# Plain attention with a second, transposed score product in place of transposes of P, and batches pipelined

## The reference

```python
h = _layernorm(x, ln1_g, ln1_b)
q = (h @ Wq).reshape(Bb, Ss, H, Dh)      # k and v alike
scores = jnp.einsum('bqhd,bkhd->bhqk', q, k) / jnp.sqrt(jnp.float32(Dh))
attn = jax.nn.softmax(scores, axis=-1)
ctx = jnp.einsum('bhqk,bkhd->bqhd', attn, v).reshape(Bb, Ss, Dd)
x = x + ctx @ Wo
m = _layernorm(x, ln2_g, ln2_b)
...
probs = jax.nn.softmax(xt @ Wg, axis=-1)          # 8 experts, the best 2 of them
h1 = jax.nn.gelu(jnp.einsum('td,edf->etf', xt, W1) + b1[:, None, :])
ye = jnp.einsum('etf,efd->etd', h1, W2) + b2[:, None, :]
...
return x + moe_out                                 # then a last layer norm
```

## Time and profile before

| | us |
|---|---|
| median of 3 runs | 3999.53 (3998.75 to 3999.96) |
| span of the profiled execution, the one time given of it | 4001.5 |
| PE busy | 2997.8 (75%) |
| PE weight loads | 1922.9 (48%) |
| DVE busy | 2299.1 (57%) |
| ACT busy | 1970.1 (49%) |
| POOL busy | 912.2 (23%) |

### The profile page before, as it was taken

One profiled execution on the slowest core, in us unless ns is written; L12 is line 12 of the kernel. 1 busy time (PEld: TensorE's weight loads), 2 busy tenths in 40 slices (PEclk: granted clock), 3 DMA queues, 4 the chain that ended last, 5 costly groups with the idle time before them and its releaser, 6 DMA issues. The chain is left out here.

```text
span 4001.5 us, 63435 instructions
## 1 busy us (share of the span) xinstructions
PE 2997.8 (75%) x19516; PEld 1922.9 (48%) x19517; DVE 2299.1 (57%) x5064; ACT 1970.1 (49%) x3070; POOL 912.2 (23%) x614
## 2 busy tenths in 40 slices
PE   4757676676757575859779797887979079999990
PEld 2434334343434353437556575655757045556560
DVE  5868586868676777746566565665656211111116
ACT  3838484857566575725446464554645022222220
POOL 3525252625343534400000000000000410000006
PEclk7565656555655555555555656556565589999995
DMA  1010010101010101050000000000000410000005
GB/s 43 11 21 18 14 25 8 31 7 33 7 32 7 32 2 38 1 204 8 19 10 17 12 11 18 11 17 8 15 16 8 149 45 29 29 27 28 29 26 169
DMA packets 124051, 123.84 MB, mean 31 GB/s; under 512 B 28737, under 2 KB 116434, under 8 KB 123730
## 3 DMA queue, kind: packets, MB, share of 16 engines
q1 hardware_dynamic: 116578, 102.46, 9.5%
q0 software_dynamic: 6144, 16.79, 1.3%
q10 hardware_dynamic: 1008, 0.54, 0.0%
HBM read 46.22 MB, written 35.65 MB: 20 GB/s over the span
## 5 line engine op out<-in xcount | busy, mean ns | idle before, releaser
L369 POOL TENSOR_TENSOR TT<-MC,TT 128x1280 f32<-128x1280 f32 x112 | 341.2, 3082 | 269.6 <-ACT TT L404 269.6
L1034 PE MATMUL PTPb<-ident,PR 128*128 128x128 f32 x1376 | 381.1, 431 | 3.1 <-ACT PR L962 3.1
L962 ACT ACTIVATE PR<-sP,nm 128x512 f32<-128x512 f32 x512 | 348.3, 683 | 36.5 <-DVE nm L1136 34.3
L1136 DVE TENSOR_REDUCE nm<-sP 128x1 f32<-128x512 f32 x512 | 346.3, 680 | 32.6 <-PE sP L1026 32.6
L1141 DVE TENSOR_TENSOR PLb<-PTPb,PHb 128x512 f16<-128x512 f32 x344 | 237.9, 691 | 200.3 <-ACT PHb L968 200.0
L521 PE MATMUL SeP<-STG 48*128 48x128 f16 (+3 forms) x512 | 227.0, 443 | 144.7 <-DVE mn L705 141.1
L1026 PE MATMUL sP<-STGb 48*128 48x512 f16 x512 | 302.8, 600 | 40.5 <-DMA STGb<-HIb 40.4
L511 PE MATMUL mP<-STG 48*128 48x512 f16 (+3 forms) x512 | 179.4, 452 | 193.8 <-DVE MC L694 105.1
L968 ACT ACTIVATE PHb<-PTPb 128x512 f16<-128x512 f32 x344 | 205.5, 597 | 233.4 <-PE PTPb L1034 232.7
L705 DVE CUSTOM_DVE_ANT_0 TT<-SeP,TT 128x128 f32<-128x128 f32 (+3 forms) x512 | 248.2, 491 | 125.6 <-PE SeP L523 110.5
L1034 PEld LDWEIGHTS PTPb<-ident,PR 128*128 128x128 f32 x1376 | 244.4, 215 | 149.2 <-issue 137.6
(11 more groups left out here) (270 smaller groups left out, 7016.0 us busy)
## 6 DMA issues: line engine op xcount, KB each, us to landing
rows_scratch<-PR SPq DMA_DIRECT2D x1, 9216.0 KB, 28.6
X<-rows_scratch SPq DMA_DIRECT2D x72, 128.0 KB, 2.0
results_scratch<-X SPq DMA_DIRECT2D x72, 128.0 KB, 1.7
STG<-HI SPq DMA_DIRECT2D x128, 64.0 KB, 2.3
STG<-HI SPq DMA_DIRECT2D x256, 32.0 KB, 2.0
STG<-LO SPq DMA_DIRECT2D x256, 32.0 KB, 2.0
W1S<-in_L_ffn_W SPq DMA_DIRECT2D x8, 1024.0 KB, 16.7
W2S<-in_L_ffn_W SPq DMA_DIRECT2D x8, 1024.0 KB, 11.9
```

The lines of the kernel that those rows point to most:

```text
L369: pool.tensor_tensor(TT[:, g % 2, j, :], MC[:, g % 2, j, :], TT[:, g % 2, j, :], ALU.add).then_inc(sum_ready, 1)
L962: act.activation(PR[:, tc % RING, :], sP[tc % 4][:, :], ACT.Exp, bias=nm[:, tc % RING:tc % RING + 1]).then_inc(bp_ready, 1)
L1034: mm = pe.transpose(PTP[tc % 3][:, k * P:(k + 1) * P], PR[:, tc % RING, k * P:(k + 1) * P], ident[:, :])
L1136: dve.tensor_reduce(nm[:, tc % RING:tc % RING + 1], sP[tc % 4][:, :], AX.X, ALU.max, negate=True).then_inc(nm_ready, 1)
```

## The change

All of the second stage is written anew, and a few lines of the third.

- Row tiles are counted through all batches. One written-out loop over slots (n) on every engine takes the place of the loops over batches. A step is TP = 8 slots and belongs to two heads, one in each half of the partitions; 64 steps are 512 tiles. Every slot has one score product for the maxima and, LAG = 40 slots later, one transposed score product. The other work of a batch stands at fixed steps and slots before or after its tiles (`USES`, `at_batch`): norm 1 at step -13 to -11, q and k at -8 and -7, staging at -6 to -4, v at -2, the output product at 18 to 20, norm 2 at 22, the router at 24. A batch's steps are eight, so these fall among the tiles of other batches.
- The score product (48 rows) only serves the row maximum (DVE). Per group of four heads (16 slots), PE transposes the 16 columns of maxima, DVE divides them by 256 and splits them into two float16 rows, and SP writes them to DRAM and from there as two more rows below q in STG, opposite rows of 256 below k. The transposed product then has AUG = 50 rows, k as stationary and q moving, and gives scores less the maximum with the keys in the partitions. ACT's exponential of it writes PT, the transposed P, as float32. There is no transpose of P and no splitting into float16 parts.
- The product with v has blocks of PT (128x128 float32) as stationary operand and v (float32, 17 columns) moving, one logical product a block, in four bursts of 16 products a group, at slots 0, 2, 4 and 6 of every second step.
- All of SP's staging is twelve DMAs a batch by way of a copy of the parts in DRAM. The high and low parts of q and k are made on POOL out of a float32 copy by ACT. Norm 1's and norm 2's gain and bias are applied by ACT on the transposed rows (per partition), in the third stage too, where the copy of the transposed rows becomes two instructions.
- SP issues the 9 MB of zeros behind the staging of batch 0. W1's load moves from the second stage's start to the third's, ahead of W2's.

The diff, cut to its core (most removed lines are in the listing above):

```diff
--- before.py
+++ after.py
@@ -779,90 +779,111 @@
 
 
 
-        W1S = sb(top, "W1S", [P, E, CH, F])
         LG = sb(top, "LG", [P, N, E])
-        w1_loaded = sem("w1_loaded")
+        gcol = sb(top, "gcol", [P, 4, CH])
         with ExitStack() as ctx:
+            NP = H // 2
+            TP = 2 * NT
+            PAIRS = B * NP
+            GROUPS = B * NG
+            TILES = PAIRS * TP
+            LAG = 5 * TP
+            AUG = R3 + 2
+            SHIFT = 256.0
+            RT = NT // 2
+
...
+            VS = sb(ctx, "VS", [P, 2, NT, H, 32])
+            PT = sb(ctx, "PT", [P, 4, 2, NT, T])
...
+            shift_d = nc.dram_tensor("shift_scratch", [2, 2, 2 * TP, P], F16, kind="Internal").ap()
+            planes_d = nc.dram_tensor("planes_scratch", [2, 2, 2 * CH, P, T], F16, kind="Internal").ap()
...
+            BEGIN = slot(-15, 0)
+            END = slot(NP * (B - 1) + 26, 0)
+
...
+            USES = [("h", 0, -11, 0), ("h", 1, -11, 4), ("q", 0, -8, 1), ("q", 1, -8, 5), ("q", 2, -7, 1), ("q", 3, -7, 5),
+                    ("v", 0, -2, 0), ("v", 1, -2, 4), ("y", 0, 18, 2), ("y", 1, 18, 6), ("w", 0, 19, 4), ("w", 1, 20, 0),
+                    ("m", 0, 23, 0), ("m", 1, 23, 4), ("l", 0, 24, 7)]
...
+                    for n in range(BEGIN, END):
+                        g = at_group(n, 2, 7)
+                        if g is not None:
+                            sp.wait_ge(nmr_done, g + 1)
+                            b, p0 = g // NG, 2 * (g % NG)
+                            if g >= 2:
+                                sp.wait_ge(shifted[g % 2], 32 * (g // 2))
+                            sp.dma_start(shift_d[g % 2].rearrange("r c t -> c r t"), NMR[:, g % 2, :, :]).then_inc(nm_stored, 16)
+                            sp.wait_ge(nm_stored, 16 * (g + 1))
+                            for par in range(2):
+                                row = 64 * par + R3
+                                sp.dma_start(STG[row:row + 2, b % 2, 0, p0:p0 + 2, :],
+                                             shift_d[g % 2, :, TP * par:TP * par + TP, :].rearrange("r (q i) t -> r q (i t)", q=2)).then_inc(shifted[g % 2], 16)
+                        b = at_batch(n, -6, 0)
+                        if b is not None:
+                            if b >= 2:
+                                sp.wait_ge(staged[b % 2], 192 * (b // 2))
+                            sp.wait_ge(blo, 4 * b + 4)
+                            sp.dma_start(planes_d[b % 2, 0].rearrange("u p t -> p u t"), HI[:, :, :]).then_inc(pl_stored, 16)
+                            sp.dma_start(planes_d[b % 2, 1].rearrange("u p t -> p u t"), LO[:, :, :]).then_inc(pl_stored, 16)
+                        for half in range(2):
...
+                                par = half
+                                for jj, planes in [(0, (0, 0)), (1, (0, 1)), (2, (1, 0))]:
+                                    for qk in range(2):
+                                        src = planes_d[b % 2, planes[qk], 2 * qk:2 * qk + 2].rearrange("c (hh r d) t -> r d (c hh) t", r=2, d=D)
+                                        dst = 64 * par + D * jj
+                                        sp.dma_start(STG[dst:dst + D, b % 2, qk, :, :], src[par]).then_inc(staged[b % 2], 16)
+                                if b == 0 and half == 1:
+                                    sp.dma_start(xs_d.rearrange("s p c -> p s c"), Z[:, :].unsqueeze(1).broadcast_to([P, SLOTS, C])).then_inc(zeroed, 16)
...
+                    pool.memset(VS[:, :, :, :, :].rearrange("p s i h d -> p (s i h) d")[:, :, D:32], 0.0).then_inc(b_set, 1)
+                    pool.memset(Z[:, :], 0.0).then_inc(b_set, 1)
+                    for par in range(2):
+                        pool.wait_ge(b_set, 2 + par)
+                        pool.memset(STG[64 * par + 32:64 * par + 64, :, 1, :, :], SHIFT).then_inc(b_set, 1)
+                    pool.wait_ge(b_set, 4)
+                    pool.memset(VS[:, :, :, :, :].rearrange("p s i h d -> p (s i h) d")[:, :, D:D + 1], 1.0).then_inc(b_set, 1)
...
+                                    pool.wait_ge(pl_stored, 32 * b)
+                                pool.wait_ge(bank_out, nth["q", u, b] + 1)
+                                pool.tensor_copy(HI[:, u, :], QF[:, u, :]).then_inc(bhi, 1)
+                                pool.wait_ge(bhi, 4 * b + u + 1)
+                                pool.tensor_tensor(LO[:, u, :], QF[:, u, :], HI[:, u, :], ALU.subtract).then_inc(blo, 1)
...
+                        if 0 <= x < TILES:
+                            p, kt, par = x // TP, x % TP // 2, x % 2
+                            if x % TP == 0 and p >= 4:
+                                act.wait_ge(av_full, (p - 4) // 2 + 1)
+                            act.wait_ge(t_full, x + 1)
+                            act.activation(PT[:, p % 4, par, kt, :], tP[x % 3][:, :], ACT.Exp).then_inc(exp_done, 1)
...
+                    for n in range(BEGIN, END):
+                        if 0 <= n < TILES:
+                            p, i, par = n // TP, n % TP // 2, n % 2
+                            b, q = p // NP, p % NP
+                            if n % (NP * TP) == 0:
+                                pe.wait_ge(staged[b % 2], 192 * (b // 2 + 1))
+                            if n >= 2:
+                                pe.wait_ge(max_done, n - 1)
+                            base = 64 * par
+                            pe.matmul(sP[n % 2][:, :], STG[base:base + R3, b % 2, 0, q, i * P:(i + 1) * P],
+                                      STG[base:base + R3, b % 2, 1, q, :], start=True, stop=True).then_inc(s_full, 1)
+                        x = n - LAG
+                        if 0 <= x < TILES:
+                            p, kt, par = x // TP, x % TP // 2, x % 2
+                            b, q = p // NP, p % NP
+                            if x % (2 * TP) == 0:
+                                g = p // 2
+                                pe.wait_ge(shifted[g % 2], 32 * (g // 2 + 1))
+                            if x >= 3:
+                                pe.wait_ge(exp_done, x - 2)
+                            base = 64 * par
+                            pe.matmul(tP[x % 3][:, :], STG[base:base + AUG, b % 2, 1, q, kt * P:(kt + 1) * P],
+                                      STG[base:base + AUG, b % 2, 0, q, :], start=True, stop=True).then_inc(t_full, 1)
+                        g = at_group(n, 2, 6)
+                        if g is not None:
+                            pe.wait_ge(max_done, 2 * TP * (g + 1))
+                            if g >= 3:
+                                pe.wait_ge(by_ready, g - 2)
+                            if g >= 1:
+                                pe.wait_ge(nmr_done, g)
+                            pe.transpose(avP[0:2 * TP, 0:P], NM[:, g % 2, :], ident[:, :]).then_inc(nmt_full, 1)
+                        for kt in range(NT):
+                            g = at_group(n, 7, 2 * kt)
+                            if g is None:
+                                continue
+                            b = g // NG
+                            if kt == 0:
+                                pe.wait_ge(nmr_done, min(g + 3, GROUPS))
+                                if g >= 1:
+                                    pe.wait_ge(by_ready, g)
+                                if g % NG == 0:
+                                    pe.wait_ge(bank_out, nth["v", 1, b] + 1)
+                                pe.wait_ge(exp_done, 2 * TP * (g + 1))
+                            for j in range(G):
+                                for key in range(NT):
+                                    mm = pe.matmul(avP[:, kt * P + 32 * j:kt * P + 32 * j + D + 1],
+                                                   PT[:, (2 * g + j // 2) % 4, j % 2, key, kt * P:(kt + 1) * P],
+                                                   VS[:, b % 2, key, G * (g % NG) + j, 0:D + 1], start=(key == 0), stop=(key == NT - 1))
+                            if kt == NT - 1:
+                                mm.then_inc(av_full, 1)
+                        for kind, i, step, t in USES:
+                            b = at_batch(n, step, t)
+                            if b is None:
+                                continue
+                            u = nth[kind, i, b]
+                            if u >= 2:
+                                pe.wait_ge(bank_out, u - 1)
...
+                    for n in range(BEGIN, END):
+                        if 0 <= n < TILES:
+                            p, i, par = n // TP, n % TP // 2, n % 2
+                            g = p // 2
+                            if n % (2 * TP) == 0 and g >= 2:
+                                dve.wait_ge(nmt_full, g - 1)
+                            dve.wait_ge(s_full, n + 1)
+                            col = TP * par + NT * (p % 2) + i
+                            dve.tensor_reduce(NM[:, g % 2, col:col + 1], sP[n % 2][:, :], AX.X, ALU.max,
```

(24 more changed lines are left out.)

526 lines of the change are left out of this document (224 added, 302 removed).

## The result

| | median, us | lowest to highest | runs |
|---|---|---|---|
| before | 3999.74 | 3998.75 to 4002.38 | 4 |
| after | 4128.83 | 4121.32 to 4135.52 | 4 |

The change makes the kernel slower: ratio 1.0323, 95% interval 1.0308 to 1.0338. The forecast was 4165 us, 4.1% slower; it came to 3.2%, inside the range. The profiled execution of the new kernel has a span of 4119.6 us.

What follows compares the result with a forecast made beforehand. Bound by PE in the tile loop at half clock and by serial batch ends. 1765 + 31 + 1488 + 22 - 31 = 3275 us against 3115; 4001.5 + (3275 - 3115) + 5 = 4166.5, so 4165 us; range 4035 to 4330.

Steps and rivals of the forecast that it cites:

- The fp32 products at 213 ns: Attention's products with v on PE: each instruction costs its weight load, 213 ns, 17 columns hidden; 109.2 us a batch.
- The rival of 242 ns: Products with v: the 17 columns add to the loads, 242 ns each, 117 us more, 4280 us; chance 0.10.
- The clock: PE in the second stage: granted clock stays at 0.50, apart from short rises after projections worth 2 us a batch.
- The batch: Second stage: a steady batch takes 186 us against 171.5 before; eight batches 1488 us.
- the 11 us that the slack was to hide: Steps without fp32 products: 3.5 us of PE slack each hides about 11 us a batch of projections.
- Row halves overlap: Neighbouring scores on different row halves overlap, 0.51 us a slot; rival without overlap 128 us more, 4290 us, chance 0.17.
- Head: Start of the second stage: first score at 1765 us, before at 1770.2; memsets some 15 us.
- Fill: Second stage's first 40 slots, without transposed scores: 31 us.
- Tail: End of the second stage, up to the logits: as before, 21 us, say 22.
- Third stage: W1's load moved there is hidden, but shares DMA engines with the scatter: 5 us added (0 to 20).
- The rival of the full clock: Tile loop at full clock: some 110 us a batch, about 3560 us; decides the sign from about 0.6; chance 0.10.
- Everything hides: Second stage: PE never waits and halves overlap fully, 172.3 us a batch, 4055 us; chance 0.15.

Runs made afterwards that it cites:

- e7: New kernel with the long products of the projections (q and k, v, output) issued in two parts, two slots apart; 4169.95 us, ratio 1.0394 to the kernel before.
- e5: New kernel with each fp32 product moving 64 columns (v's 32 columns twice) instead of 17; 3985.64 us in one run, 0.9939 of the kernel before.
- e3: New kernel with only the tile order changed, so neighbouring slots use the same half of PE's rows; 4202.98 us, ratio 1.0507 to the kernel before.
- e1: New kernel with each fp32 product moving 128 columns (v's 32 columns four times) instead of 17; 3706.31 us, ratio 0.9259 to the kernel before.
- e4: New kernel's order with the old split arithmetic: three float16 products in place of each fp32 one; 3597.49 us, ratio 0.8991 to the kernel before.
- e2: New kernel with PT and v in float16, one float16 product a block, low halves left out; 3360.37 us in one run.
- e6: Kernel before with only W1's load moved to the third stage; 3991.91 us beside 4010.13, ratio 0.9956.

## Why the prediction was right, and where its terms were off

The steady batches side by side, in us (mean granted clock of the stretch in the fourth column; e7 and e5 are of the group whose kernel before took 4010):

| kernel | a batch | at full clock | clock | kernel's time |
|---|---|---|---|---|
| e7, 17 columns, projections parted | 186.8 | 19.8 | 0.55 | 4170 |
| e3, 17 columns, same half | 188.0 | 22.5 | 0.56 | 4203 |
| after, 17 columns | 177.3 | 30.0 | 0.58 | 4129 |
| e5, 64 columns | 155.5 | 57.3 | 0.68 | 3986 |
| e1, 128 columns | 125.7 | 98.4 | 0.89 | 3706 |
| e4, float16 in three parts | 113.8 | 27.3 | 0.62 | 3597 |
| e2, float16 in one part | 85.1 | 23.2 | 0.64 | 3360 |

- **The fp32 products at 213 ns: right.** 3,289 of the 3,971 intervals inside the bursts are 200 to 220 ns, and 548 of the others 100 to 120, at the full clock; the 4,096 instructions are as counted. That the 17 columns don't show is right too: not even 64 do (e5). The rival of 242 ns is out. The Trainium skill (TensorE: Matmul & The Clock Gate, "Part 3: Packing small matmuls") states that a weight load overlaps a matmul in flight only when its row group differs; with all products on the same rows, 64 columns left the 213 ns as they were (e5), which does not agree. The section also lets a load into a background weight buffer be pulled ahead, which the prediction left out and which would fit.
- **The clock: right in kind, mis-sized.** The step "apart from short rises after the projections, worth 2 us a batch" failed. The clock is full for 30.0 us of a batch, not for a few. On the products alone that is worth 548 short intervals x 0.101 us / 8 = 6.9 us a batch, and up to the other 22 us on projections, transposes and scores, as far as PE sets the pace there. One step of a batch, with the same instructions in two batches of the new kernel, shows the rate:

```profile
2223.25:2263.78 40.53, 40.53 (x152) 30.70 (x151) 6.81 (x15) 4.65 (x9) 2.91 (x3) 0.51 0.00 1
2404.76:2439.60 34.84, 34.84 (x153) 24.73 (x152) 6.81 (x15) 4.65 (x9) 2.91 (x3) 0.60 0.01 1
```

  It is 5.7 us shorter with 6.3 us more at full clock (0.5 and 6.8), so 0.9 us for each. How much full clock there is changes with the place of the projections among the tiles (e7) and with the columns behind the loads (e5, e1).
- **The batch: 177.3 us, not 186, and partly by luck.** Two errors of opposite sign meet here. A batch has four steps with products and four without. With products they take 135.0 us, 13.1 of them at full clock; at 0.9 us each that is 147 us at the half clock (an estimate), and my terms for them come to 146 (109.2 + 16.3 + 4 + 3, and 13.6 of projections that stand there). Without products they take 42.2 us, but with 17.0 us of full clock in them. My terms for them, all at the half clock, come to 41.6 (30.4, and 22.2 - 11 of projections), so by the same 0.9 us these steps would be up to 16 us longer at the half clock than I had them. One of the four shows it: two pairs of long products and the router stand in it, my terms give about 15 us, and in e7, where it had no full clock, it took 17.8, for 13.7 in the new kernel. So the terms for the steps without products were too low, the 11 us that the slack was to hide first among them, and the clock that I had left out covered them and more. How the shortfall divides among these terms is open. (The parts named for such a step, 8 x 0.68, 1 and 0.67 us, come to 7.1 us and not to 7.6, which makes my terms for it smaller still.) PE's idle time in the five batches:

```profile
L1099 PE MATMUL avPb<-VS,PT 128*128 128x17 f32 x2561 | 514.3, 356 | 13.2 <-DVE NMR L1181 11.7 <-ACT PT L1001 1.5
L1075 PE MATMUL tP<-STGb 50*128 50x512 f16 x320 | 116.7, 548 | 2.9 <-ACT PT L1001 2.9
L1063 PE MATMUL sP<-STGb 48*128 48x512 f16 x322 | 116.2, 538 | 18.0 <-DVE NM L1172 18.0
```

  Ahead of the products it is 13.2 us, 2.6 a batch for my 3: right in size, but behind the two rows of maxima that DVE makes (L1181) and not behind an exponential. The 18.0 us behind DVE's maxima stand in the steps without products. The slots beside products cost a little less than I had: two of them 7.90 - 6.82 = 1.08 us with the changes between half and all rows, for my 1.27, 3 us a batch.
- **Row halves overlap: right,** and fuller than I put it. On the timeline two scores of different halves start as one entry (x2, 0.61 us for both), the two transposed ones 0.40 us later: 0.80 us for two slots, which is 0.40 each, just under my lower bound of 0.43, and not 0.51. With three quarters of the alternation gone (e3) the kernel takes 74 us more, a little over half of it for the overlap; I had 128 for no overlap at all.
- **Head: 1765 forecast, 1774.3 measured.** The timeline of the new kernel:

```profile
1719.59 13.89 POOL L950 MEMSET STGb<- 32x8192 f16 x2
...
1733.89 0.43 DVE L1155 BATCH_NORM_STATS2 bstb<-X 128x6 f32<-128x256 f32 x1 [16.88 <-POOL VS L952]
...
1758.46 5.53 SPq L934 DMA_DIRECT2D STGb<-planes_scratch  x12
...
1774.28 0.61 PE L1063 MATMUL sP<-STGb 48*128 48x512 f16 x2 [11.74 <-DMA STGb<-planes_scratch]
```

  The memsets cost about what I gave them (16 us, for 15), and the first statistics start at 1733.9 us, 3 later than my terms have it. What I hadn't priced is the last step: twelve loads of staging issued in 5.5 us, and then 10 us from the last issue to the first score. The page has 6.8 us as the median landing of these 128 KB loads; at that point the 9 MB of zeros had just been issued as well (35.6 us to landing), and no run shows whether they slow the staging.
- **Fill: 41.7 us, not 31,** for the first 40 slots (1774.3 to 1816.0 us, first transposed score at 1816.3): the projections of the first batches stand in them.
- **Tail: 28.6 us, not 22,** from the last product to the logits, at a clock of 0.62.
- **Third stage: 1 us, not 5:** 4119.6 - 3232.3 = 887.3 us, for 886.5 before. The load of W1 raised the DMA share in the scatter from 0.29 to 0.71, and the scatter was not longer for it. That the load also left the head was in my text as the reason for an earlier first score; on the old kernel it brought the first score forward by 14 us (e6), and the longer head took that back.
- **The sum:** 4166.5 (before I rounded it) + 9 (head) + 11 (fill) - 70 (8 x 8.7, batches) + 7 (tail) - 4 (third stage) = 4119.5, against a span of 4119.6 and a median of 4128.8.
- **The rival of the full clock** was priced at 3560 us, 110 us a batch; e1 comes to 125.7 us at 0.89, so the price was of the right size; the kernel as written doesn't get there. The point from which it decides, "about 0.6", was too low: between 0.58 (4129) and 0.68 (3986) the line crosses 4000 near 0.67. The Trainium skill (the same page, "Why this matters for your kernels") advises keeping TensorE busy without a pause to get the fast clock; 96% busy at 0.58 does not agree.
- **Everything hides** (4055 us): half true. It assumed halves that fully overlap, which they do beside products, and no waits, of which 6.9 us a batch remained.

What the kernel lost is thus one term: 32 fp32 instructions a burst whose cost is a weight load. Everything else in the change, with the split kept, is a gain of 403 us. e4 beats the kernel before by 10% and the new one by 13%; e2 is faster still, at the price of the low halves.

## What to carry to other kernels

Count the stationary operands by type before turning a product round: an fp32 block of 128x128 with 17 columns behind it cost 426 ns here at the half clock, a float16 one 27 ns, and the split into high and low halves that it was meant to save fits on DVE and ACT, which were busy 28% and 27% of the time in the new kernel. When a change has a gain and a loss of several hundred us each, build the half-way version (e4): it was the fastest of those that keep the high and the low parts, and the medians of the two kernels alone hid that. And read the granted clock beside the busy share: a PE that was 96% busy here ran at 0.58 of its clock, and with as many instructions at 0.89 (e1) a batch took 126 us for 177.

## What the runs showed that I had not expected

- More columns made the kernel faster: with 17, 64 and 128 moving behind the same loads the clock of the steady stretch was 0.58, 0.68 and 0.89, and the time 4129, 3986 and 3706 us.
- Reordering the same instructions (e7) took 58 us of full clock from the stage, and by the ratios the kernel takes 28 us more.
- Scores that stand in the order score, transposed score, score, transposed score in the program start as score, score, transposed, transposed on the timeline (2501.37 and 2501.77 us, x2 each): a product on the other half of the rows is recorded as starting ahead of the one in front of it, whose own half is still busy. By these starts PE's queue is not as strictly in order as the section on the chip has it. The Trainium skill (TensorE: Matmul & The Clock Gate, "Step-by-step: what each phase is for") says that only weight loads are pulled ahead and that matmuls stay in program order; by the recorded starts this trace does not agree.
- The exponential took 602 ns from a bank without a bias per row, which is 41 us of ACT over 512 tiles, on an engine that didn't matter here. No run changes the bias alone.
